# Diagonal products of two heads in one matmul, their blocks read out by ScalarE and VectorE and added by GpSimd

## The reference

```
h = layernorm(x) * (1 + ca) + sa
xBCzA = h @ in_proj_w.T                      # 512 -> 1024 + 2*512 + 1024 + 64
x, B, C = silu(conv4(xBC));  dt = softplus(A_log)
y = chunked scan:                            # per chunk of tokens, per head
    Y_diag = (C B^T * exp(segsum(-dt))) X    # inside the chunk
    states = B^T (decay * X);  S = decayed S + states
    Y_off  = exp(A_cum) * (C S)              # from the chunks before
x = x + ga * ((y + D*x/dt) * silu(z)) @ out_proj_w.T
h = layernorm(x) * (1 + cb) + sb
x = x + gb * (h @ (sign(w) * mean|w|).T + bias)
```

## Time and profile before

| | us |
|---|---|
| median of 3 runs | 667.58 |
| the profiled execution, its own time | 668.28 |
| its span in the profile | 666.5 |
| TensorE matmul busy | 617.1 (93%) |
| VectorE busy | 520.8 (78%) |
| ScalarE busy | 377.2 (57%) |
| GpSimd busy | 356.5 (53%) |

### The profile page before, as it was taken

How to read it: one execution, slowest core, us unless ns; L and a number is a source line. 1 busy time by engine, 2 the same in 40 slices (tenths; PEclk the granted TensorE clock), 3 DMA queues, 4 the chain that set the end, 5 groups by cost and what they waited for, 6 DMA issues and landing times.

```text
span 666.5 us, 21236 instructions
## 1 busy us (share of the span) xinstructions
PE 617.1 (93%) x8345; PEld 485.4 (73%) x8345; DVE 520.8 (78%) x947; ACT 377.2 (57%) x830; POOL 356.5 (53%) x411
## 2 busy tenths in 40 slices
PE   2786788999999999999999999999988999999995
PEld 1464666877877777877777787787866867888884
DVE  6799898987787887787877868778698376687766
ACT  2775535446555545645554664656664427665555
POOL 4775212437446363654643655547565656767652
PEclk9897998999999999999999999999997999999999
DMA  8743120343221231322222253232324634544411
GB/s 288 224 163 115 48 80 13 121 127 97 75 72 37 102 104 54 103 91 66 69 69 89 71 163 117 70 109 66 101 69 135 197 127 134 160 141 126 127 48 63
DMA packets 59866, 70.52 MB, mean 106 GB/s; under 512 B 13972, under 2 KB 33460, under 8 KB 59256
## 3 DMA queue, kind: packets, MB, share of 16 engines
q1 hardware_dynamic: 59768, 69.17, 32.5%
HBM read 54.45 MB, written 14.70 MB: 104 GB/s over the span
## 4 chain that ended last, share of the span: by engine, by line
PE 76%; DVE 12%; issue 4%; POOL 4%; ACT 3%; POOLq 0%; DVEq 0%; ACTq 0%
PE bank L1197 35%; PE bank L1963 11%; PE pair L1262 7%; PE bank L1206 4%; PE bank L1996 3%; PE pair L1235 3%; PE bank L1292 2%; DVE m_cv L1447 2%; PE bank L1215 2%; PE pair L1248 2%; DVE m_M L1477 1%; PE pair L1275 1%; POOL h_lo L431 1%; DVE chain L591 1%; DVE chain L598 1%
## 5 line engine op out<-in xcount | busy, mean ns | idle before, releaser
L1447 DVE SCALAR_TENSOR_TENSOR m_cv<-bank,gpc,m_cv 128x511 f32<-128x511 f32 (+2 forms) x192 | 143.3, 747 | 35.2 <-ACT m_cv L1354 30.7
L1197 PE MATMUL bank<-h_hi,w_hi 128*128 128x512 f32 x384 | 164.5, 428 | 4.1 <-DVE m_xs L1468 2.9
L1197 PE MATMUL bank<-h_hi,w_lo 128*128 128x512 f32 x384 | 152.3, 397 | 0.0
L1197 PE MATMUL bank<-h_lo,w_hi 128*128 128x512 f32 x384 | 152.0, 396 | 0.0
L1366 ACT ACTIVATE m_M<-bank 128x512 f32<-128x512 f32 x128 | 76.1, 595 | 68.4 <-PE bank L1206 66.7
L1354 ACT ACTIVATE m_cv<-bank,gpc 128x512 f32<-128x512 f32 x96 | 72.0, 751 | 75.0 <-PE bank L1197 74.4
L1592 POOL TENSOR_TENSOR m_S<-m_S,m_cd 128x128 f32<-128x128 f32 x96 | 39.8, 414 | 133.4 <-DVE m_S L1510 72.2
L1197 PEld LDWEIGHTS bank<-h_hi,w_hi 128*128 128x128 f32 x384 | 73.5, 191 | 24.9 <-issue 5.9
L1582 POOL TENSOR_TENSOR m_Xw<-m_Xp,wend 128x256 f32<-128x256 f32 x64 | 39.7, 621 | 85.5 <-ACT m_Xp L1374 85.5
L1197 PEld LDWEIGHTS bank<-h_hi,w_lo 128*128 128x128 f32 x384 | 72.9, 190 | 17.2
L1197 PEld LDWEIGHTS bank<-h_lo,w_hi 128*128 128x128 f32 x384 | 73.6, 192 | 11.7
(11 more groups left out here) (181 smaller groups left out, 1245.5 us busy)
## 6 DMA issues: line engine op xcount, KB each, us to landing
m_ea<-ea_scratch SPq DMA_DIRECT2D x32, 256.0 KB
m_dd<-dd_scratch SPq DMA_DIRECT2D x32, 256.0 KB
y_scratch<-m_t SPq DMA_DIRECT2D x16, 512.0 KB, 3.3
h_lo_place<-y_scratch SPq DMA_DIRECT2D x16, 512.0 KB, 4.9
p_wm<-in_L_wmod_dram SPq DMA_DIRECT2D x6, 1024.0 KB, 7.4
m_wraw<-in_L_attn_in_proj_w_dram SPq DMA_DIRECT2D x18, 256.0 KB, 3.2
w_lo_place<-in_L_attn_input__dram SPq DMA_DIRECT2D x16, 256.0 KB, 4.8
out_dram<-t_o SPq DMA_DIRECT2D x16, 256.0 KB, 2.3
```

Of the source, the lines that this page charges most:

```text
L1197: ins = pe.matmul(A[k % 3][:, :], w[:, t, kc, :], h[:, n % NB, kc, :], start=(m == 0), stop=(m == 11))
L1447: ins = dve.scalar_tensor_tensor(out=cv[:, k % 3, lag:], in0=A[k % 3][:, 0:L - lag], scalar=s.gpc[:, gp, o:o + 1], in1=cv[:, k % 3, lag:], ...
```

## The change

Five things change together.

1. `diagonal` multiplies the strip of two heads (32 columns of `Xp`, now without zeros) by the matrices of both heads (128 columns of `M`). That gives four blocks, of which two are wanted. 16 matmuls of 128 columns stand in place of 32 of 64. The wanted rows are picked at reading by a column of ones and zeros, `own_half`, made once by VectorE from the identity.
2. ScalarE gets `take_own`: it copies the first head's blocks (128x256) of both banks to `y2`, times the mask. `collect` on VectorE waits for it, and adds the second head's blocks times the mask (a scalar_tensor_tensor for the tensor_tensor). `update` waits for `take_own` too.
3. GpSimd gets `sum_own`, two adds of 128x512 elements per step, `y2` into `t1`. `sum_up` moves behind them.
4. In PSUM the wide results take the place of gram, which moves to the bank `GB`; the turned B moves to `XT`. TensorE's order in slot 0 becomes diagonal, gram q=0, offdiagonal q=1, states, offdiagonal q=0, gram q=1, the last behind a wait for the first gram (`g_first`). `turn_b` waits for `spread` of its unit, and the pieces of slot 3 for `copy_b`.
5. The last weight: ScalarE's Abs also sums each row (`accum_out`), so bn_stats and bn_aggr fall away. VectorE makes `w >= 0` once; times two minus one is applied by ScalarE's copy of the turned piece, and the second tensor_scalar falls away. The clearing of `Xp` on GpSimd (L472) and ScalarE's wait for it fall away.

```diff
@@ tensor
+                pe.wait_ge(xp_done, u + 1)
+                pe.transpose(XT[:, 2 * P:3 * P], Bt[:, n % 2, tok(u)], s.ident[:, :]).then_inc(bt_done, 1)
...
             def diagonal(u):
                 wait(pe, y1_done, u)
+                wait(pe, y2_done, u)
                 pe.wait_ge(s_new, n_new(u, 1))
                 pe.wait_ge(m_done, 2 * u + 2)
                 pe.wait_ge(xp_done, u + 1)
                 for q in range(2):
-                    for e in range(2):
-                        for j in range(4):
-                            for c in range(2):
-                                half, h = slice(64 * c, 64 * c + 64), 2 * j + e
-                                ins = pe.matmul(YS[32 * j:32 * j + 32, c, q * Q:(q + 1) * Q], Xp[half, u % 2, HG * q + h, :],
-                                                M[half, u % 2, q, h * Q:(h + 1) * Q], start=(e == 0), stop=(e == 1))
+                    for j in range(4):
+                        for c in range(2):
+                            half, first = slice(64 * c, 64 * c + 64), q * P + 32 * j
+                            ins = pe.matmul(YS[32 * j:32 * j + 32, c, 2 * P * q:2 * P * q + 2 * Q], Xp[half, u % 2, first:first + 32],
+                                            M[half, u % 2, q, 2 * j * Q:2 * (j + 1) * Q], start=True, stop=True)
...
+            def gram(u, q):
+                n, group = u // UPS, slice(64 * q, 64 * q + 64)
+                if q == 1:
+                    pe.wait_ge(g_first, u + 1)
...
+                ins.then_inc((g_first, g_done)[q], 1)
@@ scalar
+            def take_own(u):
+                n, i = u // UPS, u % UPS
+                act.wait_ge(yd_done, u + 1)
+                act.wait_ge(yo_done, u + 1)
+                act.wait_ge(st_done, min(u + 2, NU))
+                if i % 2 == 0:
+                    wait(act, t3_done, 2 * n - 2 + i // 2 + 1)
+                act.activation(y2[:, 2 * i:2 * i + 2, :, :].rearrange("p c q s -> p (c q) s"), own(0),
+                               ACT.Identity, scale=s.own_half[:, 0:1], bias=0.0).then_inc(y2_done, 1)
...
+                act.activation(s.wabs, raw_of(NWO // 2 + r), ACT.Abs, accum_out=s.wsum[:, r:r + 1]).then_inc(s.w_abs, 1)
@@ vector
             def collect(u):
-                dve.wait_ge(yd_done, u + 1)
-                dve.wait_ge(yo_done, u + 1)
-                dve.wait_ge(g_done, min(u + 2, NU))
+                dve.wait_ge(y2_done, u + 1)
...
-                dve.tensor_tensor(dst[:, first:, :, :], own[:, first:, :, :], dst[:, first:, :, :], ALU.add).then_inc(y1_done, 1)
+                dve.scalar_tensor_tensor(out=flat[:, 2 * first:, :], in0=own(1)[:, 2 * first:, :], scalar=s.own_half[:, 1:2],
+                                         in1=flat[:, 2 * first:, :], op0=ALU.mult, op1=ALU.add).then_inc(y1_done, 1)
             def update(u, c):
-                wait(dve, yd_done, u)
-                dve.wait_ge(g_done, u + 1)
+                wait(dve, y2_done, u)
             def signs(r):
-                dve.bn_stats(s.wsta[:, r % 2, :], s.wabs).then_inc(s.w_stats, 1)
-                dve.bn_aggr(s.wmv[:, r % 2, :], s.wsta[:, r % 2, :]).then_inc(s.w_mean, 1)
-                dve.tensor_scalar(raw, raw, 0.0, 2.0, ALU.is_ge, ALU.mult).then_inc(s.w_step, 1)
-                dve.tensor_scalar(s.wdiag[:, r, :], s.ident[:, :], s.wmv[:, r % 2, 0:1], None, ALU.mult).then_inc(s.w_diag, 1)
-                dve.tensor_scalar(raw, raw, -1.0, None, ALU.add).then_inc(s.w_sign, 1)
+                dve.tensor_scalar(raw, raw, 0.0, None, ALU.is_ge).then_inc(s.w_sign, 1)
+                dve.tensor_scalar(s.wdiag[:, r, :], s.ident[:, :], s.wsum[:, r:r + 1], 1.0 / D, ALU.mult, ALU.mult).then_inc(s.w_diag, 1)
@@ gpsimd
+            def sum_own(n, half):
+                m = slice(half * NC // 2, (half + 1) * NC // 2)
+                total = t1[:, :, :].rearrange("p q (m s) -> p q m s", s=Q)[:, :, m, :]
+                pool.wait_ge(y2_done, UPS * n + 2 * half + 2)
...
+                pool.tensor_tensor(total, total, y2[:, m, :, :].rearrange("p m q s -> p q m s"), ALU.add).then_inc(t3_done, 1)
...
                 if v >= 4 and m == 0:
+                    sum_own(done, 1)
+                    sum_up(done, 0)
                     sum_up(done, 1)
                 if 0 <= v + 1 < NU:
                     fade(v + 1, 1)
...
                 if v >= 0 and i == UPS - 1 and n < LAST:
-                    sum_up(n, 0)
+                    sum_own(n, 0)
```

More of the change, by code:

```diff
@@ L9 @@
 ACT = mybir.ActivationFunctionType
+AX = mybir.AxisListType
 P = 128
@@ L520, in vector @@
             normalize(i)
+        dve.wait_ge(konst, 3)
+        dve.tensor_reduce(s.own_half[:, :], s.ident[:, :].rearrange("p (j e d) -> p e j d", e=2, d=HD), AX.XY, ALU.add)
         dve.wait_ge(gpc_half, 1)
@@ L1232, in offdiagonal @@
                     for j in range(2):
-                        for q in range(2):
-                            group, strip = slice(64 * q, 64 * q + 64), slice(64 * j, 64 * j + 64)
-                            ins = pe.matmul(YS[strip, q, P + Q * c:P + Q * c + Q], S[group, (2 * u + c - 1) % 4, strip],
-                                            Ct[group, n % 2, chunk(u, c)], start=True, stop=True)
-                ins.then_inc(yo_done, 1)
+                        strip = slice(64 * j, 64 * j + 64)
+                        ins = pe.matmul(YS[strip, q, P + Q * c:P + Q * c + Q], S[group, (2 * u + c - 1) % 4, strip],
+                                        Ct[group, n % 2, chunk(u, c)], start=True, stop=True)
+                if q == 0:
+                    ins.then_inc(yo_done, 1)
             def states(u):
@@ L1247, in states @@
                         half, group = slice(64 * c, 64 * c + 64), slice(64 * q, 64 * q + 64)
-                        ins = pe.matmul(YS[group, c, 256:384], BTs[half, group], Xw[half, q, :], start=True, stop=True)
+                        ins = pe.matmul(YS[group, c, 384:512], BTs[half, group], Xw[half, q, :], start=True, stop=True)
                 ins.then_inc(st_done, 1)
@@ L1313, in tensor @@
                     if sl == 0:
+                        more = 0 <= v + 1 < NU
                         if v >= 0:
                             diagonal(v)
-                            offdiagonal(v)
-                        if 0 <= v + 1 < NU:
+                        if more:
+                            gram(v + 1, 0)
+                        if v >= 0:
+                            offdiagonal(v, 1)
+                        if more:
                             states(v + 1)
-                        if 0 <= v + 1 < NU:
-                            gram(v + 1)
+                        if v >= 0:
+                            offdiagonal(v, 0)
+                        if more:
+                            gram(v + 1, 1)
                     if sl == 2 and u < NU:
@@ L1417, in scalar @@
                         start.end_copy(act, 1)
+                    if sl == 1 and v >= 0:
+                        take_own(v)
                     for k in due(slot, {t: 1 for t in range(NT)}):
```

103 lines of the change are left out of this document (52 added, 51 removed).

## The result

The changed kernel takes 663.87 us (median of 4 runs, 662.74 to 664.0), the kernel before 667.66 us in the same series. The ratio is 0.9937 with a 95% interval of 0.9921 to 0.9954: faster, by 3.8 us where 10.4 were forecast. The profiled execution took 662.74 us with a span of 661.0, 5.5 us less than that of before.

What follows compares the result with a forecast made beforehand. TensorE was taken to bound 138 to 490 us. -7.6 - 1.15 + 0.3 + 0.9 - 2.8 = -10.35 us took the profiled 668.28 to 657.9, median 657.2; the 8-in-10 range was 651 to 666.

Steps and rivals of the forecast that it cites:

- The diagonal group: TensorE, start of slot 0: 16 wide products take 0.56 us instead of 0.78, 0.22 us off per unit.
- One reading beside it: Trace of the old diagonal group: 32 records begun in 0.28 us, read as twice the pace of 24.4 ns per matmul.
- The rest of slot 0: TensorE behind the diagonal: stream unchanged, 0.02 us per unit charged for the second gram's wait and an added semaphore.
- Units that are not first in a step: 38 of units 6 to 56: VectorE has room, so all 0.20 us counts, 7.6 us in all.
- The late `weigh` in 17, 33 and 49: GpSimd's weigh after step starts with pieces: TensorE waits some 0.3 us, three times, cost 0.9 us.
- First units of a step: 13 units with a longer VectorE chain: gain 0.15 us in five, 0.05 in eight with pieces, 1.15 us in all.
- VectorE's own new form I take as equal: VectorE: scalar_tensor_tensor in place of tensor_tensor costs the same; 0.3 us charged together with take_own's effects.
- that delay in unit 15: take_own behind a piece's two copies: VectorE's update comes 1.2 us later, hidden by a 1.95 us hole.
- The third rival: GpSimd's four adds late for fade once a step, deciding above 1.33 us per add: 15 us slower, 672; chance 0.10.
- The last weight: Units 58 to 60: shorter signs on VectorE, unit 58 at full clock; 2.8 us faster, bounds 0 and 5.
- the pieces' wait for `copy_b` come after work that in the units I looked at ended 0.1 to 0.5 us earlier: nothing: TensorE's weight pieces waiting for ScalarE's copy of the turned B: no cost.
- Units 0 to 6: Units 0 to 5, 88 to 138 us: TensorE's own work does not set the end; -0.20 us up to unit 7.

Runs made afterwards that it cites:

- half_columns: Changed kernel with each of the 16 diagonal products cut from 128 to 64 columns, leaving out the second head's blocks: 657.29 us.
- order_old: Changed kernel with slot 0 behind the diagonal ordered offdiagonal 1, offdiagonal 0, gram 0, states, gram 1: 668.52 us.
- own_first: Changed kernel with ScalarE's take_own put ahead of the copies of a weight piece: 661.6 us.
- plain_collect: Changed kernel with VectorE's collect without the mask, a plain copy and a tensor_tensor: 663.02 us.
- wait_added: Kernel before with only the last weight's edits, plus the wait of slot 3's weight pieces for ScalarE's copy of the turned B: 667.85 us.
- own_tail: Changed kernel with take_own ahead of the pieces' copies and, in unit 60, GpSimd's low_y ahead of the second gate product: 660.42 us.
- weight_alone: Kernel before with only the last weight's edits: 664.16 us.

## Why the prediction was wrong

The direction and the core of the mechanism were right, the size was not: 10.4 us forecast, 3.8 measured (5.5 in the profiled executions). By the table the missing 4.9 us are 2.75 in the first units of a step, 1.3 up to unit 7, 0.2 in the other units and 0.7 in units 61 and 62. Step by step:

- **The diagonal group**: right. 0.60 us measured, 0.56 forecast. Columns count in the wide form (37 ns for 128 columns), the number of instructions in the narrow one (24 ns). One reading beside it was off: the earlier trace rows have 32 records, thus 16 products, in 0.28 us, 17.5 ns each, which is 1.4 times the mean pace and not twice. The Trainium skill, "TensorE: Matmul & The Clock Gate", section "Wait — 56ns, not 53.3ns?", has about 25 ns between starts as a floor; this agrees with 24 ns in half_columns and 24.7 before, but the 0.40 us that it would give for 16 wide products, an estimate by that page, was 0.60.
- **The rest of slot 0**: charged at 0.02 us, costs 0.05 us in units with two states and -0.01 in the third unit of a step. With the diagonal's 0.03 us less, 25 units gain 0.14 us each and not 0.20. The wait for the first gram is indeed over in the new order; in order_old slot 0 is 0.15 us longer for it. "TensorEngine Tiling (Array Packing)" of the Trainium skill, Gotcha 1, says that different row tiles can't access one PSUM bank at the same time; the 0.15 us are the price of the wait that the kernel has for it, and no run here leaves the wait out.
- **Units that are not first in a step**: -6.01 us in 37 of them; the forecast had -6.2. That they agree is partly luck. Gains of 0.14 us in 25 units and 0.20 in 12 make 5.9 us, where 7.4 were forecast, and unit 26 alone is 0.4 us longer than before (with a wait of 0.32 us for a DMA). Against that stand costs of 0.45 us where 1.2 were charged, and 1.2 us that came unforeseen, in the eight units whose slot 0 had been long before. The late `weigh` in 17, 33 and 49 was seen rightly, at 0.15 us of slot 0 rather than 0.3; but its cause lay also in take_own's place (own_first), not in the sums and TensorE's pace alone.
- **First units of a step**: this step failed. It read the slack in a unit without pieces (0.21 us between silu and projection) and gave all of them a gain, 0.05 us each even with pieces, -1.15 us in all; measured +1.60. The sentence that failed is "VectorE's own new form I take as equal": both masked forms cost 0.06 to 0.07 us more than what they replace, in a chain without slack (the copy that became a tensor_scalar is not mentioned at all). Eight units lost 0.12 us each instead of gaining 0.05, and without the mask they are level with before, so even then there was nothing to gain (plain_collect). Three more, 12, 28 and 44, lost 0.25 us through take_own behind the pieces and GpSimd's sums (own_first). The prediction had looked at that delay in unit 15, followed it along VectorE, and called it hidden; it had not followed it into GpSimd's queue.
- **The third rival** (four adds late for fade) was thus true in three units of thirteen, at an add of 1.27 us, below my threshold of 1.33, because the adds started late rather than lasted long.
- **The last weight**: -2.8 forecast, and units 57 to 60 gave exactly -2.80. That is a coincidence of two errors: alone the part is worth -4.9 us in units 57 to 62, beside the diagonal part 2.4. Of the 2.5 us between, wait_added shows 2.0 for the pieces' wait for copy_b by itself. The lower clock in unit 58 comes beside it (1.56 us by own_first and own_tail, its cause open), and how the two share the loss is not shown. The other step that failed is "the pieces' wait for `copy_b` come after work that in the units I looked at ended 0.1 to 0.5 us earlier: nothing". It was read in units with projections and applied to units without any. Unit 58 at full clock, which I had counted on, came in weight_alone (5.87 us), not in the changed kernel (8.34 us at 0.80).
- **Units 0 to 6**: priced at nothing. VectorE sets their pace, so a faster TensorE waits longer: ahead of unit 6, 1.98 us instead of 1.58, and unit 6 itself ran at a mean clock of 0.79 and lasted 7.97 us instead of 6.69. This is the +1.14 us: unit 0 starts 1.5 us later than before (89.39 and 87.86), but at unit 6 the two kernels are level again (137.48 and 137.62), since VectorE holds both. The start of unit 0 varies between 86.8 and 90.3 us over the kernels, also where the code up to it is the same.

The sum with these values: -6.0 + 1.6 - 2.1 + 1.1 = -5.4 us, the profiled difference.

## What to carry to other kernels

When one engine is at 100% and gets faster, ask for each class of units (first, middle, last, with and without side work) which other chain is next, and read its slack there, not in one typical unit. A semaphore wait that comes with moving a buffer into another bank is free only where work stands between its two ends; look for the stretch where that work has run out. An operand added to a VectorE instruction in a chain without slack has its price every time, 0.06 to 0.07 us here.
